# A feed-forward in groups: one bounding pass instead of a scaling and a clamping pass, and another order of the second-layer groups

## What is computed

```python
NUM_GROUPS, EPS, QB = 5, 1e-5, 128.0

def _quantize_activations_groupwise(x):        # x: images x tokens x features
    gs = x.shape[0] // NUM_GROUPS              # 16 // 5 = 3 images of 256 tokens
    xq = jnp.zeros_like(x)                     # the 16th image stays zero
    for g in range(NUM_GROUPS):
        ag = x[g * gs:(g + 1) * gs]
        gamma = jnp.max(jnp.abs(ag))
        xq = xq.at[g * gs:(g + 1) * gs].set(jnp.clip(ag * QB / (gamma + EPS), -QB + EPS, QB - EPS))
    return xq

h = quantize(x @ sign(W1 - group means).T + b1)      # 96 -> 384 features
h = gelu(h, approximate=False)
out = quantize(h @ sign(W2 - group means).T + b2)    # 384 -> 96 features
t = t + out
```

## Time and profile before

| | us |
|---|---|
| median of the runs | 907.92 (lowest 903.99, highest 910.07, of 3) |
| the profiled execution, its own time | 904.23 |
| its span | 902.4 |
| mean granted clock of TensorE | 0.932 of full speed |
| VectorE busy over the span | 613.7 (68%) |
| ScalarE busy over the span | 557.1 (62%) |
| GpSimd busy over the span | 273.1 (30%) |

### The profile page before, as it was taken

How to read it: one execution, slowest core, us unless ns; L and a number is a source line. 1 busy time by engine, 2 the same in 40 slices (tenths; PEclk the granted TensorE clock), 3 DMA queues, 4 the chain that set the end, 5 groups by cost and what they waited for, 6 DMA issues and landing times.

```text
span 902.4 us, 17695 instructions
## 1 busy us (share of the span) xinstructions
PE 789.0 (87%) x5450; PEld 600.5 (67%) x5450; DVE 613.7 (68%) x1554; ACT 557.1 (62%) x1365; POOL 273.1 (30%) x536
## 2 busy tenths in 40 slices
PE   0866699999999899999997874489999978999997
PEld 0852487877778685777775564257777757777775
DVE  6325577666767354878776599357878853778875
ACT  0102276777777455888876641357888854788885
POOL 9000345555664442121211000101221210243344
PEclk9998699999999786999999887789999987999999
DMA  6000000111110121323332000123333320332220
GB/s 194 1 0 1 0 2 10 19 19 19 17 15 16 27 62 54 102 80 100 87 87 70 1 1 0 41 82 90 97 81 101 84 56 6 77 79 45 63 69 18
DMA packets 63271, 44.47 MB, mean 49 GB/s; under 512 B 34416, under 2 KB 55280, under 8 KB 63088
## 3 DMA queue, kind: packets, MB, share of 16 engines
q1 hardware_dynamic: 63216, 43.78, 19.1%
HBM read 12.24 MB, written 3.21 MB: 17 GB/s over the span
## 4 chain that ended last, share of the span: by engine, by line
PE 77%; DVE 12%; issue 3%; POOL 2%; ACT 2%; DMA 1%; SPq 1%; POOLq 0%; DVEq 0%; ACTq 0%
PE ps L978 12%; PE ps L808 10%; PE ps L878 9%; PE ps L1133 7%; PE ps L1122 7%; PE ps L815 5%; PE ps L819 4%; PE ps L827 3%; PE ps L828 2%; PE ps L840 2%; DVE xn L1187 2%; PE ps L849 2%; PE ps L870 2%; PE ps L763 1%; POOL onn L376 1%
## 5 line engine op out<-in xcount | busy, mean ns | idle before, releaser
L530 ACT ACTIVATE ee<-ps,nmax 128x128 f32<-128x128 f32 (+1 forms) x584 | 207.7, 445 | 14.9 <-DVE nmax L1272 10.9
L978 PE MATMUL ps<-w,ee 128*128 128x128 f32 x960 | 141.1, 275 | 3.2 <-ACT big L517 0.9
L978 PEld LDWEIGHTS ps<-w,ee 128*128 128x128 f32 x960 | 111.6, 142 | 24.7 <-issue 11.1
L1272 DVE TENSOR_REDUCE nmax<-ps 128x2 f32<-128x256 f32 x200 | 101.8, 550 | 35.1 <-PE ps L819 34.3
L517 ACT ACTIVATE big<-ps 128x512 f32<-128x512 f32 (+1 forms) x192 | 97.1, 549 | 22.4 <-PE ps L978 22.1
L1572 DVE TENSOR_TENSOR hhl<-ee,hhl 128x512 fp32r<-128x512 f32 x96 | 80.4, 844 | 29.7 <-ACT hhl L719 28.3
L1269 DVE TENSOR_REDUCE nmax<-ps 128x4 f32<-128x1024 f32 x48 | 58.8, 1225 | 59.3 <-PE ps L808 59.2
L808 PE MATMUL ps<-kh,big 128*128 128x256 f32 x384 | 94.2, 389 | 1.2 <-ACT ee L530 1.2
L878 PE MATMUL ps<-big,vh 128*32 128x256 f32 (+1 forms) x1188 | 92.2, 353 | 0.0
L1122 PE MATMUL ps<-qk,w1hl 128*128 128x512 f32 x288 | 84.8, 405 | 0.4 <-DVE ee L1575 0.4
L461 POOL TENSOR_TENSOR xc<-big,xc 96x512 f32<-96x512 f32 x32 | 52.3, 1634 | 107.0 <-DVE big L1566 106.9
(11 more groups left out here) (247 smaller groups left out, 1373.9 us busy)
## 6 DMA issues: line engine op xcount, KB each, us to landing
qk<-hl SPq DMA_DIRECT2D x288, 96.0 KB, 3.1
big<-moe_gate SPq DMA_DIRECT2D x8, 768.0 KB, 6.8
w<-w_in SPq DMA_DIRECT2D x1, 1735.5 KB, 13.3
xc<-x_in SPq DMA_DIRECT2D x4, 384.0 KB, 6.5
l_mix<-on SPq DMA_DIRECT2D x32, 48.0 KB, 2.1
tok<-l_mix SPq DMA_DIRECT2D x16, 96.0 KB, 2.0
out<-xc SPq DMA_DIRECT2D x8, 192.0 KB, 2.1
w<-w_in SPq DMA_DIRECT2D x1, 998.0 KB, 9.7
```

What stands on the lines that cost most here:

```text
L530: last = nc.scalar.activation(ee[:, ke, hh, qc, 0:w], src, ACT.Exp, bias=nmax[:, kp, hh, qc:qc + 1])
L978: last = nc.tensor.transpose(ps[:, 4 + hh, b * P:(b + 1) * P], ee[:, u, hh, qc, tc * P:(tc + 1) * P], ident)
L1272: last = V.tensor_reduce(out=nmax[:, kp, :, qc], in_=ps[:, 2 * kp:2 * kp + 2, qc * N:qc * N + scores_cols(l, qc)], axis=AX.X, op=ALU.max, ...
```

## The change

Two edits in one diff.

The quantisation of the first layer keeps the values unscaled: they are clamped from above and below in one VectorE pass, to plus and minus (maximum + EPS) x (128 - EPS) / 128, and the Gelu on ScalarE reads its input with the scale 128 / (maximum + EPS), a value per partition in SBUF. Two operations on one element per partition are added to compute the two bounds, and a small tile `bound` holds the lower one.

The hand-written orders of TensorE and VectorE change. TensorE now runs `y0` ahead of `h3` and `y1` ahead of `h4`; VectorE now takes `y0` ahead of `a3`, and `y1` and `f0` ahead of `a4`. ScalarE's order stays.

```diff
-F2_PE = ["h0", "h1", "h2", "h3", "y0", "h4", "y1", "y2", "y3", "y4"]
+F2_PE = ["h0", "h1", "h2", "y0", "h3", "y1", "h4", "y2", "y3", "y4"]
 F2_ACT = ["c0", "c1", "c2", "e0", "c3", "e1", "c4", "e2", "e3", "e4"]
-F2_DVE = ["a0", "a1", "q0", "a2", "q1", "a3", "q2", "y0", "a4", "q3", "y1", "f0", "q4", "y2", "f1", "y3", "f2", "y4", "f3", "f4"]
+F2_DVE = ["a0", "a1", "q0", "a2", "q1", "y0", "a3", "q2", "y1", "f0", "a4", "q3", "y2", "f1", "q4", "y3", "f2", "y4", "f3", "f4"]
...
+        bound = sb("bound", [P, NG])
...
                             act.wait_ge(sg("f2_quant"), g + 1)
-                            nc.scalar.activation(y1[:, :, g * GT:(g + 1) * GT], y1[:, :, g * GT:(g + 1) * GT], ACT.Gelu).then_inc(sg("f2_gelu"), 1)
+                            nc.scalar.activation(y1[:, :, g * GT:(g + 1) * GT], y1[:, :, g * GT:(g + 1) * GT], ACT.Gelu,
+                                                 scale=amax[:, 0, g:g + 1]).then_inc(sg("f2_gelu"), 1)
...
                         elif what == "q":
                             quant_scale(0, g)
+                            top, low = amax[:, 1, g:g + 1], bound[:, g:g + 1]
+                            link(V.tensor_scalar(top, top, (QB - QEPS) / QB, None, ALU.mult))
+                            link(V.tensor_scalar(low, top, -1.0, None, ALU.mult))
                             v = y1[:, :, g * GT:(g + 1) * GT]
-                            link(V.tensor_scalar(v, v, amax[:, 0, g:g + 1], QB - QEPS, ALU.mult, ALU.min))
-                            V.tensor_scalar(v, v, -QB + QEPS, None, ALU.max).then_inc(sg("f2_quant"), 1)
+                            V.tensor_scalar(v, v, top, low, ALU.min, ALU.max).then_inc(sg("f2_quant"), 1)
```

## The result

| | before | after |
|---|---|---|
| median of the runs, us | 907.92 (903.99 to 910.07) | 915.53 (914.25 to 917.22) |
| ratio | | 1.0094, 95% interval 1.0059 to 1.0128 |
| the profiled execution: time, span | 904.23, 902.4 | 914.25, 912.4 |
| feed-forward stage in the profile | 57.17 | 65.62 |
| from there to the first score pass of l = 3 | 21.58 | 22.92 |

The changed kernel is slower by 0.9%; the forecast was 913.8 us, +0.65%. "The stage" is, here and in all experiments, the time on VectorE from the start of the second `a` to the first operation of the layer norm: 508.37 to 565.54 before.

The account below looks back on a forecast made before the run. VectorE was taken to bound the feed-forward. 6.75 us of its work goes, but its idle time rises from 1.0 to 13.8 us; laid out in time, +5.9 us, so 907.92 + 5.9 = 913.8 us, range 906.5 to 918.5.

Parts of the forecast that it names:

- The step that carried the forecast: Feed-forward: `h3`, queued behind `y0`, delays `c3`, `e1` and `a3`; `a3` starts near 526.3 us instead of 521.5.
- The bounding pass: First layer's quantisation on VectorE: new pass 1.88 us, 1.35 less per group, 6.75 us of work gone; Gelu 2.20.
- Rival C: New VectorE pass goes at the reduction's pace, 2.54 us for 1.88; 2.0 us more, 915.8; chance 0.05.
- The estimate by the Trainium skill: Clamping pass on VectorE at two fp32 elements per cycle: 1.38 us, edit worth about 1.0 us a group; not used.
- The waits: VectorE idle in the feed-forward for `y0`, ahead of `a3`, then for `y1`, `y2`, `y4`: 13.8 us against 1.0 before.
- the low clock: TensorE's `y0`, `y1`, `y2`, `y4` each slowed after idle waits of 2.8 us or more: 5.86 us instead of 4.23.
- Rival B: TensorE's clock falls deeper, whole burst and part of the `h` behind at 1.2 GHz; 4.2 us more, 918.0; chance 0.12.
- The stages behind: From the layer norm after the feed-forward onward: unchanged, TensorE having been idle before them in both kernels.
- A: Rival: TensorE stays at 2.4 GHz through `y0`, `y1`, `y2`, `y4`; 6.5 us off, 907.3, not slower; chance 0.12.
- D: Rival: VectorE remains the feed-forward's bound and the new order hides all waits; 902.1 us; chance 0.03.

Follow-up runs that it names:

- Experiment 3: Changed kernel with TensorE's list alone put back, VectorE's list left new; stage 52.98 us, median 903.89 us, ratio to before 0.9972.
- Experiment 4: Changed kernel with ScalarE's list matched to the new order (`e1` ahead of `c3`, `e2` ahead of `c4`); stage 56.99 us, median 906.22 us, ratio to before 1.0006.
- experiment 1: Changed kernel with TensorE's and VectorE's lists both put back, leaving the bounding pass alone; stage 51.09 us, median 899.49 us, ratio to before 0.9943.
- 2: Kernel before with the change's two new lists only, old passes and unscaled Gelu; stage 65.91 us, median 918.15 us, ratio to before 1.0146.
- 6: Changed kernel plus matmuls with unused results on TensorE while it waits, holding the clock; stage 56.51 us, median 907.82 us, ratio to before 1.0014.
- 5: The changed kernel run again, unaltered, beside the kernel before; stage 65.68 us, median 914.77 us, ratio to before 1.0099.
- 7: Kernel before with the two new lists, old passes and unscaled Gelu, plus unused matmuls holding TensorE's clock; stage 60.30 us, median 911.17 us, ratio to before 1.0060.

## Why the prediction was right

**The path.** The step that carried the forecast was `h3` held behind `y0`, and with it `c3`, `a3`, `e1`. It was laid out to `a3` at 17.98 us behind the start of the second `a`; measured 525.69 - 507.69 = 18.00. For `a4` 30.81 were forecast and 538.45 - 507.69 = 30.76 measured. Experiment 3 shows that it is TensorE's list that costs: put back alone, it takes 12.6 us off the stage. Experiment 4 shows that it costs so much because ScalarE's list was left as it was: matched alone, that list takes 8.6 us off. The two parts overlap and don't add up.

**The bounding pass.** Forecast 1.88 us, measured 1.88; Gelu forecast 2.20, measured 2.21. The reading from two unrelated groups of small tiles held on 2304 elements. Rival C (2.54) is out.

**The estimate by the Trainium skill.** The Trainium skill, VectorE: DVE Perf Modes, section on the perf-mode tier table, led to an estimate of about 1.0 us per group and not 1.35. The pass with its two bounds took 1.88 us and `q` fell from 4.09 to 2.74, which is 1.35; the stage of experiment 1 gained 6.1 us over five groups, against the 5 of that estimate. Here the measurement decides against the page.

**The waits.** Forecast 2.7, 3.3, 2.6, 2.3 and 2.9 us; measured 2.63, 3.18, 2.40, 3.32 and 4.13. The first three are right within 0.2, the last two were forecast too small by 1.0 and 1.2.

**What was mis-sized: the low clock.** I priced each slowed burst at 5.86 us, the one price that the rows of before had. `y0` and `y1` took that, but `y4` took 7.19, and `y2` with `y3` 11.22 instead of 5.86 + 4.23, with `y2` at 7.21 on the path. That is the forecast's missing 2.5 us of the stage (65.62 against 571.48 - 508.37 = 63.11): up to `a4` the layout was exact to 0.05 us, and all of the 2.5 comes behind it. Rival B had the mechanism, at `y0`, `y1` and `y4` with 1.4 more each; it came at `y4` and at `y2`, 1.3 more each. I gave it 0.12, which was too little: the row of `h0` to `h3` that it rested on the earlier trace rows was in plain sight and showed that a longer low stretch occurs. That all four bursts would be slowed came true, but the length of the wait, from which I took it, is no rule: `y2` of before was slowed after 2.20 us, and in 2 `y1` and `y2` were not after 2.59.

**The stages behind.** "Unchanged" was right of their instructions and not of their time. From the layer norm to the first scores 22.92 us instead of 21.58, and the clock was low for longer there too: in the second row of TensorE's transposes (0.50 in the mean, 0.58 before), in the third (0.65, before 1.00), and in the first projection behind, which took 1.99 us at 0.50 instead of 1.07 at 1.00. In 6 the same stretch took 20.80.

**The rivals.** A (the clock holds, 907.3 us, level with before) did not happen, but as an experiment it did: 6 is rival A made by hand, at 907.82 us and a ratio of 1.0014, and the clock's price in the stage was 9.1 us, where A had counted 6.5. D falls with the waits: VectorE was busy for 47.75 of 65.62 us.

**The numbers.** 915.53 lies inside the range and 1.7 us above the forecast. The ratio of +0.94% is clear of no change, and its upper end passes the 1% at which I called a run slower; 0.75 on "within 1%" named the likelier side, by little. That the median came so close is in part luck. The two profiled executions differ by 10.0 us, 4.1 more than the forecast's 5.9 and as much as rival B's 5.9 + 4.2. The median of before lies 3.7 us above its profiled execution and that of after only 1.3, which takes 2.4 of the miss away. Beside each other in 5 the medians differ by 9.4.

## What to carry to other kernels

When engines run hand-written lists, moving one step in one list moves what stands behind it in all of them: lay out the first two groups in time, engine by engine, before believing that an order is "matched", and look above all at the list that was not changed. A pass removed from the bounding engine is worth its time only while that engine stays the bound: test it alone first, as here, where it gained 0.6% and lost it all to the order. And an idle wait of TensorE that an order opens can be paid for twice, once as the wait and again in the burst behind it: here the second payment was 1.6 to 3.0 us on each of four bursts, and in 2 it was nothing on two of them.

## What the runs showed of the hardware that I had not expected

The cost of an idle wait varies: the same burst of 36 instructions took 4.15 to 4.26 us at the full clock, 5.86 to 5.89 with some of it at 1.2 GHz, and 6.90 to 7.29 with most of it. After 2.6 to 2.7 us of idleness all of that happened: 4.26 (order only), 5.89 (after, `y1`), and `y2` after, with 5.9 us at 1.2 GHz. The length of the wait alone doesn't tell which; what else decides was not tried. Nor need a slowed burst begin slow: in `y1` after, the granted clock was 1.00 from 528 to 529 us, 0.70 in the next microsecond, 0.50 to 532, 0.59 to 533, and 1.00 again from there on. So a burst can pay for the wait ahead of it when it is already under way at full clock.

Far from the change the clock made differences as large as a third of the result. The gate's 64 small matmuls of the last block, some 180 us behind the feed-forward, in the changed kernel and with the clock held:

```profile
756.92 9.67 PE L1109 MATMUL ps<-w,xn 128*128 128x4 f32 x64 [0.82 <-ACT xc L701]
```

```profile
747.39 12.53 PE L1113 MATMUL ps<-w,xn 128*128 128x4 f32 x64 [0.78 <-ACT xc L701]
```

They are the same instructions. In the first, the granted clock was 1.00 for part of the time (0.74 in the mean), in the second 0.50 nearly throughout (0.56). 3 and 7 had the long form too (12.69 and 12.38 us), the other kernels the short one (9.67 to 9.97). That is perhaps where part of the stage's gain went: 6 is 9.1 us shorter than after in the stage but, by the ratios, 7.7 us in the run. Whether that belongs to the kernel or to the execution, one profile of each can't tell.

On VectorE the number of operands that hold a value per partition seems to show: 1.76 us with none (a maximum), 1.82 with one (a product and a minimum), 1.88 with two (a minimum and a maximum), all on 2304 elements. From 1.82 to 1.88 both passes have two operations, though not the same ones; from 1.76 to 1.82 a second operation comes in as well, so what is the operand's and what the operation's is not separated there.
